# A two-layer graph block on one core: weights of the second layer split straight from a PSUM bank, identity products in the tail, and a new order of head and tail

## The reference, cut to what matters

```python
# layer 0: masked attention
v, q, k = relu(x @ Wv + bv), relu(x @ Wq + bq), relu(x @ Wk + bk)
att = softmax(q @ k.T * mask - 9e15 * (1 - mask), axis=2)
x = layernorm(x + relu(att @ v @ Wo + bo))
# layer 1: additive attention
h = x @ W_w.T + W_b
e, f = h @ a1, h @ a2
u = mask * exp(e[:, :, None] + f[:, None, :] + a_b)
x = layernorm(x + (u / u.sum(2)) @ h)
```

## Time and profile before

| | us |
|---|---|
| runs shown, median of 3 (lowest, highest) | 425.09 (424.24, 425.4) |
| the profiled execution's own time | 424.09 |
| its span, first to last instruction | 422.4 |
| PE busy | 396.3 |
| DVE busy | 348.4 |
| ACT busy | 336.8 |
| POOL busy | 266.7 |

### The profile page before, as it was taken

How to read it: one execution, slowest core, us unless ns; L and a number is a source line. 1 busy time by engine, 2 the same in 40 slices (tenths; PEclk the granted TensorE clock), 3 DMA queues, 4 the chain that set the end, 5 groups by cost and what they waited for, 6 DMA issues and landing times.

```text
span 422.4 us, 8762 instructions
## 1 busy us (share of the span) xinstructions
PE 396.3 (94%) x2812; PEld 367.5 (87%) x2812; DVE 348.4 (82%) x1002; ACT 336.8 (80%) x642; POOL 266.7 (63%) x230
## 2 busy tenths in 40 slices
PE   8789999999999999999999999999999999998580
PEld 7668998899999999999999999999999989988480
DVE  4595789879869896989869996989969999898755
ACT  5375767998789896998789987998789788985753
POOL 2453446456709698497929697496929893751862
PEclk9889999999999999999999999999999999999666
DMA  8940472626781657726792657726592768226661
GB/s 290 372 151 2 139 238 71 229 60 215 276 298 52 222 190 252 285 67 215 270 326 73 225 204 257 264 81 219 199 330 71 248 184 267 100 83 184 209 174 50
DMA packets 37868, 80.71 MB, mean 191 GB/s; under 512 B 2752, under 2 KB 19264, under 8 KB 37824
## 3 DMA queue, kind: packets, MB, share of 16 engines
q1 hardware_dynamic: 37680, 80.03, 55.1%
q10 hardware_dynamic: 144, 0.14, 0.2%
HBM read 75.96 MB, written 4.19 MB: 190 GB/s over the span
## 4 chain that ended last, share of the span: by engine, by line
PE 76%; DVE 11%; ACT 3%; issue 3%; DMA 2%; POOL 1%; ACTq 0%; DVEq 0%; POOLq 0%
PE pt_ps L1415 11%; PE m_ps L1463 10%; PE av_ps L1427 7%; PE av_ps L1428 7%; PE av_ps L1429 7%; PE s_ps L1356 6%; PE s_ps L1358 6%; PE s_ps L1357 6%; PE m_ps L1363 4%; PE m_ps L1356 3%; PE m_ps L1358 3%; PE m_ps L1357 3%; DVE prob L920 3%; DMA adjt_in<-in_adj_t_dram 2%; PE m_ps L1364 2%
## 5 line engine op out<-in xcount | busy, mean ns | idle before, releaser
L622 ACT ACTIVATE prob_th<-pt_ps 128x512 fp32r<-128x512 f32 x128 | 74.5, 593 | 30.8 <-PE pt_ps L1415 30.4
L928 DVE TENSOR_TENSOR prob_tl<-pt_ps,prob_th 128x512 fp32r<-128x512 f32 x128 | 85.7, 682 | 16.2 <-ACT prob_th L622 15.8
L920 DVE CUSTOM_DVE_ANT_0 prob<-s_ps,penalty 128x1024 f32<-128x1024 f32 x64 | 78.1, 1220 | 16.4 <-issue 6.5
L614 ACT ACTIVATE prob<-prob,neg_max 128x1024 f32<-128x1024 f32 x64 | 73.5, 1149 | 14.9 <-DVE neg_max L920 14.9
L379 POOL TENSOR_SCALAR penalty<-adj_in 128x1024 bf16<-128x1024 f32 x64 | 66.6, 1053 | 15.7 <-DVE neg_max L920 9.1
L1415 PE MATMUL pt_ps<-ident,prob 128*128 128x128 f32 x512 | 74.7, 275 | 0.0
L1427 PE MATMUL av_ps<-prob_th,vh 128*128 128x256 f32 x256 | 74.4, 291 | 0.0
L1429 PE MATMUL av_ps<-prob_th,vl 128*128 128x256 f32 x256 | 72.4, 283 | 0.0
L1428 PE MATMUL av_ps<-prob_tl,vh 128*128 128x256 f32 x256 | 72.4, 283 | 0.0
L572 ACT ACTIVATE adj_t<-adjt_in 128x1024 fp32r<-128x1024 f32 x58 | 61.1, 1054 | 9.2 <-DMA adjt_in<-in_adj_t_dram 7.5
L1415 PEld LDWEIGHTS pt_ps<-ident,prob 128*128 128x128 f32 x512 | 60.1, 142 | 7.1 <-issue 0.4
(11 more groups left out here) (132 smaller groups left out, 928.4 us busy)
## 6 DMA issues: line engine op xcount, KB each, us to landing
adj_in<-in_adj_dram SPq DMA_DIRECT2D x64, 512.0 KB, 5.1
adjt_in<-in_adj_t_dram SPq DMA_DIRECT2D x64, 512.0 KB, 4.3
xt_in<-in_x_t_dram SPq DMA_DIRECT2D x16, 256.0 KB, 4.2
x_in<-in_x_dram SPq DMA_DIRECT2D x8, 512.0 KB, 4.7
out_dram<-out_sb SPq DMA_DIRECT2D x14, 256.0 KB, 5.4
out_dram<-out_sb SPq DMA_DIRECT2D x4, 128.0 KB, 1.8
wb<-in_pack_b_dram SPq DMA_DIRECT2D x1, 320.0 KB, 4.1
wa<-in_pack_a_dram ACTq DMA_DIRECT2D x1, 132.0 KB, 3.7
```

The costliest lines, as they stand in the source:

```text
L614: sc.activation(prob[i % 2][:, :], prob[i % 2][:, :], ACT.Exp, bias=neg_max[:, i:i + 1], scale=-1.0, accum_out=row_sum[b % 2][:, i:i + 1]) ...
L622: sc.activation(prob_th[n % 2][:, tiles(k), (i % 2) * P:(i % 2 + 1) * P], pt_ps[k][:, :].rearrange("p (c n) -> p c n", n=P), ACT.Copy).the ...
L920: v.tensor_tensor_reduce(out=prob[i % 2][:, :], in0=s_ps[:, :, :].rearrange("p a n -> p (a n)"), in1=penalty[:, n % RING, :], scale=-1.0, ...
L928: v.tensor_tensor(prob_tl[n % 2][at], pt_ps[k][:, :].rearrange("p (c n) -> p c n", n=P), prob_th[n % 2][at].bitcast(F32), ALU.subtract).th ...
```

## The change

**Weights of h.** The identity is now made in `rhs1[:, 0:D]` itself, so there is no `ident` tile and no copy of it; `w1h` is rounded and `w1l` subtracted directly from the bank `av_ps`, without `w1f`. `place_rhs1` has three instructions instead of four and stands before `split_vo`; `split_w1` has seven instead of eight.

**Head.** PE projects k before q, runs `scores(0, 0)` and `project_k(1, 0)` before `form_w1`, and the projections of graph 1 stand in another order. DVE, ACT, POOL and SP follow: both halves of x of graph 1 are split on POOL before `convert(0, 1)`, and `x_t` of graphs 1 and 2 is loaded earlier.

**Tail.** `hold_clock()` is new: six products of the identity with itself on PE, ahead of `aggregate_early(0)` and again ahead of `aggregate_early(1)`. `aggregate_early(3)` and `(4)` move behind some of `aggregate_last`. The aggregation of graph 5 moves ahead of the scores of graph 7, ACT rounds adjacency tiles in another order, and DVE's steps are permuted. `batch_pass` is as before.

```diff
-    SET_READ, SET_ROUNDED, SET_ALL = 4, 6, 8
+    SET_READ, SET_ALL = 5, 7
     WARM = 11
+    HOLD = 6
...
-        w1f, rhs1 = sb("w1f", [P, E1]), sb("rhs1", [P, E1])
+        rhs1 = sb("rhs1", [P, E1])
+        ident = rhs1[:, 0:D]
...
         HEAD_SLOTS = (
-            ("q", 0, 0), ("k", 0, 0), ("k", 0, 1), ("q", 0, 1), ("v", 0, 0), ("v", 0, 1),
-            ("v", 1, 0), ("q", 1, 0), ("k", 1, 0), ("q", 1, 1), ("k", 1, 1), ("o", 0, 0),
-            ("v", 1, 1),
+            ("k", 0, 0), ("k", 0, 1), ("q", 0, 0), ("v", 0, 0), ("q", 0, 1), ("v", 0, 1),
+            ("k", 1, 0), ("q", 1, 0), ("q", 1, 1), ("v", 1, 0), ("v", 1, 1), ("k", 1, 1),
+            ("o", 0, 0),
         )
...
# SP, head
                 load_adj(0, 0)
+                load_x_t(1, 0)
                 load_adj(0, 1)
+                load_x_t(1, 1)
+                load_x_t(2, 0)
                 load_adj(0, 2)
-                load_x_t(1, 0)
                 load_x(0)
-                load_x_t(1, 1)
                 load_adj(0, 3)
...
# POOL, head
                 convert(0, 0)
+                x_lo(1, 0)
+                x_lo(1, 1)
                 convert(0, 1)
-                x_lo(1, 0)
                 convert(0, 2)
+                v_lo(0, 0)
                 convert(0, 3)
...
# ACT, tail: the end of layer 1 of the last graph
                 norm0(LAST, 0)
                 round_adj(LAST - 1, 7)
+                x1_hi(LAST, 0)
                 round_adj(LAST, 0)
-                x1_hi(LAST, 0)
                 norm0(LAST, 1)
-                exp_ef(LAST, 0)
                 round_adj(LAST, 1)
                 x1_hi(LAST, 1)
-                g_hi_den(LAST, 0)
+                exp_ef(LAST, 0)
                 g_full(LAST, 0)
+                g_hi(LAST, 0)
                 round_adj(LAST, 2)
-                g_hi(LAST, 0)
                 round_adj(LAST, 3)
                 exp_ef(LAST, 1)
+                g_hi_den(LAST, 0)
                 g_hi_den(LAST, 1)
...
             def place_rhs1():
 
-                dve.wait_ge(ident_ok, 2)
-                v.tensor_copy(rhs1[:, 0:D], ident[:, :]).then_inc(rhs_ok, 1)
+                dve.wait_ge(wa_arrived, 16)
                 v.tensor_copy(rhs1[:, D:E1], wa[:, A1:A2 + 1]).then_inc(rhs_ok, 1)
...
             def split_w1():
                 dve.wait_ge(set_full, 3)
-                v.tensor_copy(w1f[:, :], av_ps[:, 0:E1]).then_inc(w1_ok, 1)
+                v.tensor_copy(w1h, av_ps[:, 0:E1]).then_inc(w1_ok, 1)
...
-                dve.wait_ge(w1_ok, SET_READ)
-                v.tensor_copy(w1h, w1f[:, :]).then_inc(w1_ok, 1)
+                dve.wait_ge(w1_ok, 4)
+                v.tensor_tensor(w1l, av_ps[:, 0:E1], w1h.bitcast(F32), ALU.subtract).then_inc(w1_ok, 1)
...
# DVE, head
                 first_x_lo(1)
+                place_rhs1()
                 split_vo()
-                first_q_lo(0)
                 first_k_lo(0)
                 first_k_lo(1)
+                first_q_lo(0)
                 v_out(0, 0)
-                place_rhs1()
                 v_out(0, 1)
                 mask_max(0, 0)
+                split_w1()
                 mask_max(0, 1)
...
# DVE, tail
-                agg_out(LAST - 1, 5)
                 residual0(LAST, 3)
                 stats0(LAST, 1)
+                agg_out(LAST - 1, 5)
                 var_eps0(LAST, 1)
                 agg_out(LAST - 1, 6)
                 agg_out(LAST - 1, 7)
-                x1_lo(LAST, 0)
                 scale_out(LAST - 1)
                 shift_mean0(LAST, 1)
+                x1_lo(LAST, 0)
...
-                g_lo_den(LAST, 0)
                 var_eps1(LAST - 1)
...
                 h_out(LAST, 7)
+                g_lo_den(LAST, 0)
                 g_lo_den(LAST, 1)
...
+            def hold_clock():
+
+                pe.wait_ge(ptl_done, 2 * T * B - 1)
+                for _ in range(HOLD):
+                    pe.matmul(pt_ps[0][:, 0:P], ident, ident, start=True, stop=True)
...
# PE, head
             def head():
-                project_q(0, 0)
                 project_k(0, 0)
                 project_k(0, 1)
+                project_q(0, 0)
+                project_v(0, 0)
                 project_q(0, 1)
-                project_v(0, 0)
                 project_v(0, 1)
+                scores(0, 0)
+                project_k(1, 0)
                 form_w1()
-                scores(0, 0)
-                project_v(1, 0)
+                project_q(1, 0)
                 scores(0, 1)
                 transpose_p(0, 0, 0)
                 transpose_p(0, 0, 1)
-                project_q(1, 0)
+                project_q(1, 1)
                 scores(0, 2)
                 transpose_p(0, 1, 0)
+                project_v(1, 0)
+                scores(0, 3)
                 transpose_p(0, 1, 1)
-                project_k(1, 0)
-                scores(0, 3)
                 transpose_p(0, 2, 0)
-                project_q(1, 1)
+                project_v(1, 1)
+                scores(0, 4)
                 transpose_p(0, 2, 1)
-                scores(0, 4)
...
# PE, tail
                 aggregate(LAST - 1, 6)
+                aggregate(LAST - 1, 7)
                 transpose_x1(LAST, 0)
-                aggregate(LAST - 1, 7)
                 project_h(LAST, 0)
...
                 project_h(LAST, 7)
+                hold_clock()
                 aggregate_early(0)
+                hold_clock()
                 aggregate_early(1)
                 aggregate_early(2)
-                aggregate_early(3)
-                aggregate_early(4)
                 aggregate_last(0)
                 aggregate_last(1)
+                aggregate_early(3)
                 aggregate_last(2)
                 aggregate_last(3)
+                aggregate_early(4)
                 aggregate_last(4)
```

More of the change, by code:

```diff
@@ L468, in head @@
                 k_lo(1, 0)
-                x_lo(2, 0)
                 k_lo(1, 1)
@@ L525, in tail @@
                 add_wb(LAST - 1)
+                convert(LAST, 6)
+                g_lo(LAST - 1, 0)
                 convert(LAST, 7)
@@ L528, in tail @@
                 norm1(LAST - 2, 0)
-                g_lo(LAST - 1, 0)
                 g_lo(LAST - 1, 1)
@@ L796, in tail @@
                 exp_ef(LAST - 2, 1)
-                q_hi(LAST, 1)
+                g_hi_den(LAST - 2)
+                g_full(LAST - 2, 1)
                 av_hi(LAST - 1, 2)
-                g_hi_den(LAST - 2)
+                g_hi(LAST - 2, 1)
                 prob_hi(LAST - 1, 7, 0)
@@ L802, in tail @@
                 probs(LAST, 0)
[L803 removed]
+                round_adj(LAST - 2, 3)
                 prob_hi(LAST, 0, 0)
[L805 to L812 removed]
+                v_hi(LAST, 0)
+                prob_hi(LAST, 0, 1)
@@ L830, in tail @@
+                probs(LAST, 4)
+                prob_hi(LAST, 3, 0)
+                av_hi(LAST, 0)
+                prob_hi(LAST, 3, 1)
+                round_adj(LAST - 1, 0)
                 round_adj(LAST - 1, 1)
                 prob_hi(LAST, 4, 0)
-                x1_hi(LAST - 1, 1)
+                exp_ef(LAST - 1, 0)
+                prob_hi(LAST, 4, 1)
+                g_full(LAST - 1, 0)
+                g_hi(LAST - 1, 0)
                 probs(LAST, 5)
-                prob_hi(LAST, 4, 1)
@@ L835, in tail @@
-                exp_ef(LAST - 1, 0)
+                av_hi(LAST, 1)
                 round_adj(LAST - 1, 2)
-                g_full(LAST - 1, 0)
-                av_hi(LAST, 1)
                 prob_hi(LAST, 5, 0)
-                round_adj(LAST - 1, 3)
-                g_hi(LAST - 1, 0)
-                exp_ef(LAST - 1, 1)
                 prob_hi(LAST, 5, 1)
                 probs(LAST, 6)
+                exp_ef(LAST - 1, 1)
+                g_hi_den(LAST - 1)
                 g_full(LAST - 1, 1)
@@ L1238, in tail @@
                 var_eps0(LAST - 1)
+                prob_lo(LAST, 1, 0)
                 agg_out(LAST - 2, 4)
+                prob_lo(LAST, 1, 1)
+                shift_mean0(LAST - 1)
+                mask_max(LAST, 3)
                 agg_out(LAST - 2, 5)
+                prob_lo(LAST, 2, 0)
+                agg_out(LAST - 2, 6)
                 mask_max(LAST, 4)
-                shift_mean0(LAST - 1)
+                x1_lo(LAST - 1, 0)
+                agg_out(LAST - 2, 7)
+                scale_out(LAST - 2)
+                x1_lo(LAST - 1, 1)
                 prob_lo(LAST, 2, 1)
-                agg_out(LAST - 2, 6)
-                agg_out(LAST - 2, 7)
-                prob_lo(LAST, 3, 0)
-                scale_out(LAST - 2)
-                mask_max(LAST, 5)
-                prob_lo(LAST, 3, 1)
-                x1_lo(LAST - 1, 0)
-                stats1(LAST - 2, 0)
                 h_out(LAST - 1, 0)
@@ L1281, in tail @@
                 prob_lo(LAST, 7, 1)
+                o_out(LAST, 2)
                 stats0(LAST, 0)
+                agg_out(LAST - 1, 1)
+                residual0(LAST, 2)
                 var_eps0(LAST, 0)
-                agg_out(LAST - 1, 1)
```

(3 more changed lines are left out.)

267 lines of the change are left out of this document (126 added, 141 removed).

## The result

The changed kernel takes 414.79 us in the median of 4 runs (414.56 to 415.3), the kernel before 424.95 us beside it (424.24 to 425.4). The ratio is 0.9764, 95% interval 0.9747 to 0.9781: 10.2 us or 2.4% faster.

A forecast was written before the change was run, and what follows sets the result against it. PE was taken to set the pace, busy 396.3 of 422.4 us. From 424.09, head 7.5, middle of the tail 0 and end 1.3 came off, giving 415.3; 0.7 added for the median made 416.0 us, range 412.5 to 420.5.

The forecast's parts named there:

- The head, 7.5 forecast: Head: PE's new order removes both gaps and the slow clock behind them, 7.5 us won, lower bound 4.4.
- the ceiling of 8.20: Head: most that can be won, two PE gaps (2.71, 2.11) plus slow-clock losses behind them (1.70, 1.68), 8.20 us.
- The first gap: Head: PE waits 2.77 us for DVE's place_rhs1 before form_w1's products at 14.46; 2.71 us counted as lost.
- The collision of `split_vo` with the first `convert`: Head: if POOL's convert came first, split_vo would end late and project_v(0, 0) wait 0.8 us; taken as 0.
- The floor of the head, 4.4: Head: lower bound, only the first gap and its slow stretch go, 2.71 + 1.70 = 4.4 us won.
- The middle of the tail, 0 forecast: Middle of the tail: late transpose_p against 0.97 us of PE idle time, taken as 0, bounds 1.0 lost to 1.0 won.
- The end of the tail, 1.3 forecast: After the last project_out: earlier g_lo 0.9, early aggregations 0.6, identity products -0.2; 1.3 us won, bounds 1.5 lost to 3.0 won.
- A gap left in the head: Rival (1), head: a gap remains and the clock falls behind it, only 4.4 us won there; 419.1 us, chance 0.19.
- a slow head: Rival (4), head: small gaps keep the clock at 1.2 GHz until the first pass; about 431 us, chance 0.04.
- the gain would be lost in the first passes: Rival (3), first passes: they wait for tiles or ACT and lose the head's gain; about 424 us, chance 0.05.
- the tail turns worse: Rival (2), tail: slow products delay a finished g_lo or the middle loses 1.0; 2.0 lost, 419.3 us, chance 0.10.
- the first two rivals: Rivals (1), a gap remains in the head, 419.1 us, chance 0.19, and (2), a worse tail, 419.3 us, chance 0.10.

The follow-up runs named there:

- place_early: Kernel before with only place_rhs1 moved ahead of split_vo; 418.91 us, ratio 0.9862 to the kernel before.
- pool_order: Changed kernel with POOL's add_wb(LAST, 1) and g_lo(LAST, 1) ahead of norm1 of graph 6, one store behind the last loads; 414.28 us, ratio 0.9754.
- no_hold_again: Changed kernel without identity products in the tail (HOLD = 0), second measurement; 416.07 us, ratio 0.9782 to the kernel before.
- head_only: Changed kernel with the tail of before on all engines and its bank slots, no identity products in the tail; 415.46 us, ratio 0.9789.
- tail_only: Kernel before with the changed tail on every engine, identity products included; 423.57 us, ratio 0.9975 to the kernel before.
- via_sbuf: Changed kernel with h's weights again copied to SBUF and split from there, at the new place in the order; 415.57 us, ratio 0.9792.
- direct_split: Kernel before with place_rhs1 ahead of split_vo and h's weights split straight from the bank at split_w1's old place; 417.41 us, ratio 0.9820.
- after_third: The changed kernel itself, unaltered, measured again beside the third group; 414.88 us, ratio 0.9758 to the kernel before.

## Why the prediction came out, point by point

**The time.** 416.0 us was forecast, 414.8 measured. Of the 1.2 us between them, the profiled execution was 0.6 below its forecast of 415.3, and the 0.7 that I put on top for the median was not there: the changed kernel's profiled execution stood 0.1 from its median.

**The head, 7.5 forecast.** Right, and by the mechanism given. Measured are 8.0 us at `scores(1, 0)` and 7.5 at `scores(7, 0)`. From the first projection it is 8.6 (46.89 and 38.26 us), over the ceiling of 8.20. The gaps were sized right: PE's idle time in this stretch fell by 4.88 us, all of it in two waits, where the ceiling has 4.82. The slow clock was sized too low: the same 258 products took 3.75 us less besides, where the ceiling has 3.38. The margin of 0.7 us that I left for small waits wasn't needed. The first gap had more behind it than I read: not one but two copies of `place_rhs1` were held, the copy of the identity too (1.11 us from 12.00, beside POOL's `x_lo` from 11.76 to 13.03), and the change drops just this one. Each mark named beforehand holds: `form_w1` without a wait; `scores(0, 0)` 5.54 us behind the first projection, where 5.5 was forecast (11.5 against 6.03); no stretch below 0.9 from the first projection to 45 us; 0.23 us of waiting in the 40 us of the middle, where over 1 us would have been a sign of being wrong; no wait for `x_lo(1, 0)`, for `mask_max(0, 2)` or for `split_vo`; the identity products from 389.67 us, with the clock rising ahead of `aggregate_last`. The collision of `split_vo` with the first `convert` was judged by a margin of 0.25 us and took place with one of 0.06, in the harmless order. In all ten profiled executions with the new head `split_vo` came first, by 0.03 to 0.15 us, so the other order, and the 0.8 us kept for it as a bound, stays unseen.

**The floor of the head, 4.4.** It was the first gap and its slow stretch, and `place_early`, which removes just these, won 5.8 (95% interval 4.3 to 7.3), with 3.6 at the head in the profiled execution. The head of the kernel before doesn't always take the same time (last section), which may be part of the difference.

**The middle of the tail, 0 forecast.** Measured 0.9, inside the bounds of 1.0 either way. From `scores(7, 0)` to the last product of `attend(7, 3)` it took 51.50 to 51.87 us in the four executions with the old order and 50.94 to 51.20 in the ten with the new one. So it is a small true gain, 0.3 to 0.9, which I had set against a loss at `transpose_p` that didn't come.

**The end of the tail, 1.3 forecast, 1.0 measured: the sum was near, and its terms were wrong.** I had 0.9 for an earlier `g_lo`, 0.6 for the early aggregations moved out of the way and -0.2 for the identity products. Times are counted here from the last product of `attend(7, 3)`. What stands ahead of `g_lo(7, 1)` did win: ACT's `g_hi` ended 19.84 us later before and 19.07 after, 0.8 earlier. But on POOL `g_lo(7, 1)` stands behind `norm1` of graph 6, and began only when that ended. Timeline of ACT in the changed kernel:

```profile
392.75 0.63 ACT L659 ACTIVATE g<-h_sb 128x512 fp32r<-128x512 f32 x1
```

Timeline of POOL, the same kernel:

```profile
393.12 1.04 POOL L438 TENSOR_TENSOR out_sb<-out_sb,rstd 128x512 f32<-128x512 f32 x1
394.12 1.29 POOL L425 TENSOR_TENSOR g<-h_sb,g 128x512 fp32r<-128x512 f32 x1
```

So `g_lo(7, 1)` ended 21.32 us later before and 21.10 after, 0.2 won and not 0.9; `pool_order`, which moves it ahead of `norm1`, has it at 20.2. That the early aggregations no longer hold `aggregate_last(0)` is so: it starts 0.7 us earlier (21.93 and 21.20). But the end didn't gain by it. `no_hold_again`, the new order without products and with the clock low, took 40.08 us and the kernel before, also low, 39.65; with the clock up the old order took 38.54 (`head_only`) and the new one 38.69. So the order, 1.5 forecast, gave -0.4 and -0.15, and the products, -0.2 forecast, gave 1.4 by the same executions and 1.2 by the medians. I had priced how long they run and how much sooner `aggregate_last` could start, and took the shorter aggregations only for what PE gains by them; they count because DVE, the limit of the end, is fed by them. Two errors of 1.4 to 1.9 us in opposite directions met in a sum that looks right: that it came within 0.3 us was luck. (Twelve records of the products took 2.87 us at the low clock, where I had 2.5.)

**The rivals.** A gap left in the head and a slow head are refuted: PE is full and the clock is 1.00 from the first projection to 45 us. (In the price of the slow head, the 9.7 us that I called slow are the two stretches; by their clock 6.8 us of them were slow.) That the gain would be lost in the first passes is nearly refuted: they gave back 0.4 of 8.0. That the tail turns worse is refuted by `tail_only`, 1.2 us faster. That adjacency tiles or rounds would hold the end took place in small: PE's last aggregations wait 0.29 and 0.60 us for ACT's `adj_t`, behind which DVE is still the last. The upper end of the range holds either of the first two rivals with a lost us more; both together would have been 422.4 us, outside of it.

## What to carry to other kernels

Look at the idle time of the engine that limits the kernel and at its granted clock together: here waits of 2.1 and 2.8 us at the head cost 3.8 us more in slow products behind them, one of 1.3 us left the clock up. When a DVE instruction of a few columns takes a microsecond, see whether it ends with an instruction of POOL; every one shown here did. Read one input from a PSUM bank or move it ahead of POOL's work, and look what else POOL's instruction then meets. Where an engine must wait near the end and others live on its output, filler products in the wait directly ahead of that output paid here; filling earlier waits too brought nothing. And read the order of the engine that makes an operand before counting on an earlier operand: a step that could begin 0.8 us sooner began 0.2 sooner, behind the work written ahead of it.

## What the runs showed of the hardware that I had not expected

- Who is held depends on who starts first. In the changed kernel POOL's `v_lo` starts at 18.67 and takes 1.30 us, and DVE's `q_lo` (19.24) is held, 1.27 us. In `via_sbuf` DVE's `q_lo` starts first (19.43) and takes 0.74, and POOL's `v_lo` (19.59) is held, 1.72 us.
- The clock can rise at a different product in two executions of one kernel, at the start too: the 22 warm-up records had brought the clock up by the first projection in the changed kernel (0.50 us for its first product), but not in `tail_only`, `place_early`, `direct_split`, `pool_order` and `no_hold_again` (0.77). With the same head, `no_hold_again` then took 38.63 us to `scores(1, 0)` and `after_third` 38.25, so a slow start costs about 0.4 us.
- In the old order such a start can cost more. In `tail_only`, whose head is that of before, `place_rhs1` came some 0.5 us later behind it; there a second `convert` of POOL followed the first, and the last copy was held as well. PE waited 3.63 us instead of 2.77, the clock averaged 0.50 instead of 0.63 from 14.40 to 19.00 us, and the head took 49.18 us instead of 46.89. That is why the span from the first projection (417.2, before 416.4) hides the gain of this kernel: from `scores(1, 0)` on it is 1.4 us shorter than before, beside 1.2 in the medians. Timeline of DVE, of POOL and of PE in `tail_only`:

```profile
14.85 1.06 DVE L1072 COPY bv_wide<-wa 128x128 f32<-128x128 f32 x1
```

```profile
13.73 2.09 POOL L380 TENSOR_SCALAR penalty<-adj_in 128x1024 bf16<-128x1024 f32 x2
```

```profile
16.05 0.77 PE L1513 MATMUL av_ps<-rhs,wb 128*128 128x130 f32 x2 [3.63 <-DVE bv_wide L1072]
```

- The first weights landed between 4.35 and 5.41 us in executions that had the same work up to there, so a comparison of two single executions at the head is good to half a microsecond at best.
